# Combining, channel mix and Gram products of a four-layer kernel merged into one stage, with row normalisations on ScalarE

## What is computed

```python
# first layer, end: experts combined, x = res + mo
out = jnp.einsum('ted,te->td', ye, wmat)
# second layer
x_prev = jnp.concatenate([jnp.zeros((B, 1, C), x.dtype), x[:, :-1, :]], axis=1)
xr = mu_r * x + (1.0 - mu_r) * x_prev
xk = mu_k * x + (1.0 - mu_k) * x_prev
r = jax.nn.sigmoid(jnp.einsum('btc,dc->btd', xr, W_r))
k_act = jnp.square(jax.nn.relu(jnp.einsum('btc,dc->btd', xk, W_k)))
out = r * jnp.einsum('btc,dc->btd', k_act, W_v)
# third layer: no softmax, so (q k^T) v = q (k^T v)
attn = jnp.einsum('bhik,bhjk->bhij', q, k)
out = jnp.einsum('bhik,bhkj->bhij', attn, v)
```

## Time and profile before

| | |
|---|---|
| median of three runs | 2536.11 us (2535.68 to 2536.63) |
| the profiled execution: time / span | 2536.58 us / 2534.9 us |
| mean granted TensorE clock | 0.847 of full |
| VectorE busy over the span | 1722.8 us (68%) |
| TensorE busy (matmul) | 1937.0 us (76%) |
| ScalarE busy | 1150.6 us (45%) |
| GpSimd busy | 1454.4 us (57%) |

### The profile page before, as it was taken

How to read it: one execution, slowest core, us unless ns; L and a number is a source line. 1 busy time by engine, 2 the same in 40 slices (tenths; PEclk the granted TensorE clock), 3 DMA queues, 4 the chain that set the end, 5 groups by cost and what they waited for, 6 DMA issues and landing times. The chain is left out here.

```text
span 2534.9 us, 35893 instructions
## 1 busy us (share of the span) xinstructions
PE 1937.0 (76%) x10268; PEld 1496.3 (59%) x10269; DVE 1722.8 (68%) x3375; ACT 1150.6 (45%) x1897; POOL 1454.4 (57%) x1018
## 2 busy tenths in 40 slices
PE   6787868696978788786399999903977686599980
PEld 2445555454545454555399999902665575599970
DVE  1788888888888888885744444466942697644438
ACT  2676767677676768674123232212511452111112
POOL 1789899899989898986133333221211440255542
PEclk9887979697978878797599999956987797699995
DMA  2111111111111111110511111151000012222216
GB/s 73 34 34 47 35 46 36 45 31 40 44 35 44 30 52 30 47 35 21 222 45 47 48 48 48 40 171 47 1 17 11 1 34 96 102 70 69 68 58 198
DMA packets 77370, 139.12 MB, mean 55 GB/s; under 512 B 10449, under 2 KB 48465, under 8 KB 76450
## 3 DMA queue, kind: packets, MB, share of 16 engines
q1 hardware_dynamic: 63586, 100.19, 11.9%
q0 software_dynamic: 13632, 37.24, 4.6%
HBM read 105.38 MB, written 32.01 MB: 54 GB/s over the span
## 5 line engine op out<-in xcount | busy, mean ns | idle before, releaser
L778 DVE TENSOR_TENSOR_SCAN a_hs<-a_dA,a_carry,a_hs 128x512 f32<-128x512 f32 x512 | 637.1, 1268 | 27.7 <-POOL a_hs L400 24.1
L400 POOL TENSOR_TENSOR a_hs<-a_u,a_b_bc 128x1024 f32<-128x1024 f32 x258 | 624.6, 2423 | 0.4
L924 PE MATMUL a_h_ps<-k_ident,a_hs 128*128 128x128 f32 x2064 | 341.1, 318 | 183.7 <-DVE a_hs L778 113.4
L924 PEld LDWEIGHTS a_h_ps<-k_ident,a_hs 128*128 128x128 f32 x2064 | 284.0, 164 | 302.4 <-DVE a_hs L778 136.2
L554 ACT ACTIVATE a_dA<-a_delta,a_a_neg 128x512 f32<-128x512 f32 x512 | 351.8, 688 | 105.0 <-DVE a_hs L778 102.6
L412 POOL TENSOR_TENSOR a_acc<-a_acc,a_part 128x512 f32<-128x512 f32 x242 | 323.6, 1337 | 70.1 <-ACT a_part L568 68.9
L743 DVE SCALAR_TENSOR_TENSOR a_acc<-a_h_ps,a_c_tok,a_acc 128x512 f32<-128x512 f32 x242 | 177.4, 733 | 109.1 <-PE a_h_ps L924 109.0
L568 ACT ACTIVATE a_part<-a_h_ps,a_c_tok 128x512 f32<-128x512 f32 x242 | 165.7, 685 | 149.8 <-PE a_h_ps L924 133.6
L1224 POOL DMA_INDIRECT expert_rows<-m0e_ys,k_pair x71 | 74.1, 1044 | 236.2 <-DVE m0e_ys L1280 225.1
L1290 DVE TENSOR_TENSOR m0e_hT<-m0e_gs,m0e_u 128x512 f32<-128x512 f32 x70 | 48.2, 688 | 185.3 <-ACT m0e_gs L1243 185.3
L1243 ACT ACTIVATE m0e_gs<-m0e_g 128x512 f32<-128x512 f32 x71 | 42.4, 597 | 268.2 <-PE m0e_u L1321 268.2
(11 more groups left out here) (431 smaller groups left out, 3779.0 us busy)
## 6 DMA issues: line engine op xcount, KB each, us to landing
a_b_bc<-b_rows SPq DMA_DIRECT2D x132, 256.0 KB, 3.2
q_y<-expert_rows SPq DMA_DIRECT2D x32, 512.0 KB, 5.6
a_xl<-in_L_attn_x SPq DMA_DIRECT2D x9, 512.0 KB, 3.5
norm_rows<-a_shared SPq DMA_DIRECT2D x9, 512.0 KB, 2.9
m0w_up<-in_m_up SPq DMA_DIRECT2D x1, 4096.0 KB, 12.2
m0w_gate<-in_m_gate SPq DMA_DIRECT2D x1, 4096.0 KB, 22.5
m0w_down<-in_m_down SPq DMA_DIRECT2D x1, 4096.0 KB, 32.2
q_xl<-in_L_attn_x SPq DMA_DIRECT2D x8, 512.0 KB, 3.5
```

Of the source, the lines that this page charges most:

```text
L400: pool.tensor_tensor(hs[n % NBUF][:, half, :], u[s][:, half, :], b_bc[:, n % NBUF:n % NBUF + 1, :].broadcast_to([P, 2, T]), ALU.mult).then ...
L778: dve.tensor_tensor_scan(hs[k][:, c, :], dA[c][:], hs[k][:, c, :], carry[:, hf, c, n:n + 1], ALU.mult, ALU.add).then_inc(s_scan, 1)
L924: last = pe.transpose(hT_ps[j % 2][:, c * P:(c + 1) * P], hs[(n - 1) % NBUF][:, c, j * P:(j + 1) * P], ident[:])
```

## The change

The combining, the channel mix and the Gram products become one stage, `mix_phase`, a written-out pipeline of 13 iterations. Iteration n combines unit n, adds it to x in n+1, transposes and mixes unit n-2, makes the products of unit n-3, and the Gram product of unit n-5. Work moves between engines:

- The weighting of the first expert's rows goes from VectorE to ScalarE (w1 y1) and GpSimd (+ H, 128x1024). The weighted sum of the second stays on VectorE.
- The normalisation for the transposes and that for the Gram products go from VectorE to ScalarE, as scale times x plus shift; GpSimd makes the shift (`NBx`).
- The difference of neighbouring tokens and the carried column go from VectorE to GpSimd.
- The PSUM tiles are halves; relu, the transposed copy, sigmoid and the multiplication go by halves; the r and v products share the PSUM tiles `v_ps`. `ka`, `sig`, `rc`, `a`, `a2` have one buffer each.
- The Gram sums start and stop with flags, the products of zeros go, and ScalarE copies the Gram matrices; the matrix stage keeps weights, mask and the chain of small products.

The core of the diff:

```diff
-def channel_mix_phase(nc, io, per, x):
...
-def attention_matrix_phase(nc, io, per, x):
+def mix_phase(nc, io, per, x, x_in, G):
+    N = TILES // TJ
+    PER_SEQ = N // B
+    LATE_A, LATE_B, LATE_G = 2, 3, 5
+    NBUF = 3
...
+            for t, n in ((w_r, "w_r"), (w_k, "w_k"), (w_v, "w_v"), (mu, "mu")):
+                sp.dma_start(t[:], io[n]).then_inc(s_w, 16)
+            yv = io["expert_rows"][0:PAIRS * P, :].rearrange("(k t p) d -> p k t d", k=2, p=P)
+            for u in range(N):
+                if u >= NBUF:
+                    sp.wait_ge(s_x["q"], u - NBUF + 1)
+                for k in range(2):
+                    sp.dma_start(y[u % NBUF][:, k], yv[:, k, u * TJ:(u + 1) * TJ, :]).then_inc(s_ld[u % NBUF], 16)
+                if u >= 2:
+                    sp.wait_ge(s_x["q"], u - 1)
+                sp.dma_start(xl[u % 2][:], x_in[:, u * TJ:(u + 1) * TJ, :]).then_inc(s_xl[u % 2], 16)
...
+            def power(out, var):
+                pool.tensor_tensor(out, var, half[:], ALU.pow).then_inc(s_pow, 1)
+                powers[0] += 1
+                pool.wait_ge(s_pow, powers[0])
+            def inverse(k, u):
+                s = u % 2
+                pool.wait_ge(s_mv[k], u + 1)
+                power(rs[k][s][:], v[k][s][:])
+                pool.tensor_tensor(nb[k][s][:], rs[k][s][:], neg[k][s][:], ALU.mult).then_inc(s_rs[k], 1)
+            def final(k, u):
+                t = slice(u * TJ, (u + 1) * TJ)
+                pool.wait_ge(s_v2[k], u + 1)
+                power(per.RS[:, t], xv[k][u % 2][:])
+                pool.tensor_tensor(NBx[:, t], per.RS[:, t], xneg[k][u % 2][:], ALU.mult).then_inc(s_fin[k], 1)
+            def difference(u):
+                s = u % 2
+                if u % PER_SEQ == 0:
+                    pool.wait_ge(s_diff, u + -1) if u >= 2 else None
+                    pool.memset(aT[s][:, :, 0:1], 0.0).then_inc(s_halo, 1)
+                else:
+                    pool.wait_ge(s_aT[1], u)
+                    pool.tensor_copy(aT[s][:, :, 0:1], aT[1 - s][:, :, T:]).then_inc(s_halo, 1)
+                for c in range(DC):
+                    pool.wait_ge(s_aT[c], u + 1)
+                if u >= 1:
+                    pool.wait_ge(s_mix, u)
+                pool.wait_ge(s_halo, u + 1)
+                pool.tensor_tensor(diff[:], aT[s][:, :, 1:], aT[s][:, :, 0:T], ALU.subtract).then_inc(s_diff, 1)
+            for n in range(N + LATE_G):
+                if has(n):
+                    pool.wait_ge(s_y0, n + 1)
+                    pool.tensor_tensor(flat(y[n % NBUF][:, 0]), flat(y[n % NBUF][:, 0]), flat(per.H[:, n * TJ:(n + 1) * TJ, :]),
+                                       ALU.add).then_inc(s_h, 1)
+                if has(n - 1):
+                    final("q", n - 1)
+                if has(n - LATE_B - 1):
+                    final("c", n - LATE_B - 1)
+                if has(n - LATE_A):
+                    difference(n - LATE_A)
+                if has(n):
+                    inverse("q", n)
+                if has(n - LATE_B):
+                    inverse("c", n - LATE_B)
...
+            def normal(out, u):
+                for q, t in enumerate(tiles(u)):
+                    last = act.activation(out[:, q, 0:D], x[:, t, :], ACT.Identity, scale=per.RS[:, t:t + 1], bias=NBx[:, t:t + 1])
+                return last
+            def scale(k, u, r):
+                s = u % 2
+                act.wait_ge(s_rs[k], u + 1)
+                for q in range(TJ):
+                    last = act.activation(r[:, q, :], r[:, q, :], ACT.Identity, scale=rs[k][s][:, q:q + 1], bias=nb[k][s][:, q:q + 1])
+                last.then_inc(s_sc[k], 1)
+            def copy_gram(b):
+                act.wait_ge(s_g, PER_SEQ * (b + 1))
+                for c in range(DC):
+                    act.activation(G[b][:, c, :], g_ps[c][:, 0:D + 1], ACT.Copy).then_inc(s_gc, 1)
+            act.wait_ge(s_c, 2)
+            for n in range(N + LATE_G):
+                ma, mb, g = n - LATE_A, n - LATE_B, n - LATE_G
+                if has(n):
+                    act.wait_ge(s_ld[n % NBUF], 32 * (n // NBUF + 1))
+                    for q, t in enumerate(tiles(n)):
+                        last = act.activation(y[n % NBUF][:, 0, q, :], y[n % NBUF][:, 0, q, :], ACT.Copy, scale=per.top[:, t, 0:1])
+                    last.then_inc(s_y0, 1)
+                if has(ma):
+                    act.wait_ge(s_fin["q"], ma + 1)
+                    normal(a, ma).then_inc(s_a, 1)
+                if has(mb):
+                    if mb:
+                        act.wait_ge(s_vp, 2 * mb)
+                    for c in range(DC):
+                        act.wait_ge(s_k, DC * mb + c + 1)
+                        act.activation(ka[:, c, :], k_ps[c][:], ACT.Relu).then_inc(s_relu, 1)
+                if has(ma):
+                    if ma >= 2:
+                        act.wait_ge(s_mix, ma - 1)
+                        act.wait_ge(s_diff, ma)
+                    for c in range(DC):
+                        act.wait_ge(s_t[c], ma + 1)
+                        act.activation(aT[ma % 2][:, c, 1:], t_ps[c][:], ACT.Copy).then_inc(s_aT[c], 1)
+                if has(mb):
+                    act.wait_ge(s_relu, DC * (mb + 1))
+                    act.activation(ka[:], ka[:], ACT.Square).then_inc(s_ka, 1)
+                    if mb:
+                        act.wait_ge(s_out, 2 * mb)
+                    for h in range(2):
+                        act.wait_ge(s_r, 2 * mb + h + 1)
+                        act.activation(sig[:, 2 * h:2 * h + 2, :], v_ps[h][:], ACT.Sigmoid).then_inc(s_sig, 1)
+                if has(g):
+                    if g == PER_SEQ:
+                        copy_gram(0)
+                    act.wait_ge(s_fin["c"], g + 1)
+                    if g:
+                        act.wait_ge(s_g, g)
+                    normal(a2, g).then_inc(s_a2, 1)
+                if has(n):
+                    scale("q", n, y[n % NBUF][:, 1])
+                if has(mb):
+                    scale("c", mb, rc)
+            copy_gram(1)
...
+            def row_stats(k, u, r):
+                for q in range(TJ):
+                    last = dve.bn_stats(st[:, q, :], r[:, q, :])
+                link(last, padded=True)
+                for q in range(TJ):
+                    last = dve.bn_aggr(agg[:, q, :], st[:, q, :])
+                link(last)
+                dve.tensor_scalar(neg[k][u % 2][:], agg[:, :, 0], -1.0, None, ALU.mult)
+                dve.tensor_scalar(v[k][u % 2][:], agg[:, :, 1], EPS_LN, None, ALU.add).then_inc(s_mv[k], 1)
+            def add(k, u, old, r):
+                t = slice(u * TJ, (u + 1) * TJ)
+                dve.wait_ge(s_sc[k], u + 1)
+                dve.tensor_tensor(flat(x[:, t, :]), flat(old), flat(r), ALU.add).then_inc(s_x[k], 1)
+                dve.wait_ge(s_x[k], u + 1)
+                link.carry_wait()
+                for q, j in enumerate(tiles(u)):
+                    last = dve.bn_stats(st[:, q, :], x[:, j, :])
+                link(last, padded=True)
+                for q, j in enumerate(tiles(u)):
+                    last = dve.bn_aggr(per.MV[:, j, :], st[:, q, :])
+                link(last)
+                dve.tensor_scalar(xneg[k][u % 2][:], per.MV[:, t, 0], -1.0, None, ALU.mult)
+                dve.tensor_scalar(xv[k][u % 2][:], per.MV[:, t, 1], EPS_LN, None, ALU.add).then_inc(s_v2[k], 1)
+            dve.wait_ge(s_w, 64)
+            for n in range(N + LATE_G):
+                ma, mb = n - LATE_A, n - LATE_B
+                if has(n - 1):
+                    u = n - 1
+                    dve.wait_ge(s_xl[u % 2], 16 * (u // 2 + 1))
+                    add("q", u, xl[u % 2][:], y[u % NBUF][:, 1])
+                if has(mb - 1):
+                    u = mb - 1
+                    add("c", u, x[:, u * TJ:(u + 1) * TJ, :], rc[:])
+                if has(n):
+                    b = n % NBUF
+                    dve.wait_ge(s_h, n + 1)
+                    for q, t in enumerate(tiles(n)):
+                        last = dve.scalar_tensor_tensor(out=y[b][:, 1, q, :], in0=y[b][:, 1, q, :], scalar=per.top[:, t, 1:2],
+                                                        in1=y[b][:, 0, q, :], op0=ALU.mult, op1=ALU.add)
+                    link(last, padded=True)
+                    row_stats("q", n, y[b][:, 1])
+                if has(ma):
+                    s = ma % 2
+                    dve.wait_ge(s_diff, ma + 1)
+                    for k, o in enumerate((xr[s], xk[s])):
+                        for c in range(DC):
+                            last = dve.scalar_tensor_tensor(out=o[:, c, :], in0=diff[:, c, :], scalar=mu[:, k, c:c + 1],
+                                                            in1=aT[s][:, c, 0:T], op0=ALU.mult, op1=ALU.add)
+                    last.then_inc(s_mix, 1)
+                if has(mb):
+                    for h in range(2):
+                        dve.wait_ge(s_sig, 2 * mb + h + 1)
```

(64 more changed lines are left out.)

235 lines of the change are left out of this document (60 added, 175 removed).

## The result

The changed kernel takes 2565.84 us (median of four runs, 2564.71 to 2567.45) against 2535.89 for the kernel before (2535.19 to 2536.63): a ratio of 1.0121, 95% interval 1.0108 to 1.0133. The predicted time was 2562.5. The profiled execution's span is 2563.1 us, 28.2 longer than before.

A forecast was written before the change was run, and what follows sets the result against it. A ring of waits through the engines' written orders, 27.9 us per full iteration with clock loss, bounds the merged stage: 256.3 plus 39.7 for the matrix stage is 296.0 against 269.5, giving 2562.5 us, forecast range 2550 to 2576 (0.64).

The forecast's parts named there:

- The ring: Merged stage: a closed chain of waits through the engines' written orders, 25.7 us per full iteration at full clock.
- A: GpSimd makes the inverse deviation and shift after the channel mix's row statistics: 2.3 us, lower end 1.4.
- E: TensorE transposes, then does the r product: 4.8 us with a hand-over, plus 2.2 us for slow clock.
- G: ScalarE normalises for the Gram product, behind the sigmoid: 2.07 us.
- H: TensorE's Gram product for one unit, ahead of the v product in its order: 3.6 us with hand-over.
- Start: Merged stage until first rows are there: 5.5 us plus 1.8 for four weight loads ahead of them, 7.3 us.
- Iterations 0 to 2: Merged stage's first iterations, with only the combining: 11.6 us each, the difference adding 2.4 in the third, 37.2 us.
- Matrix stage: Stage after the merged one: chain of products 31.1 us, exposed loads 5.8, stage switch 0.6, clock 2.2; 39.7 us.
- The clock term: TensorE's idle of about 7 us ahead of the transposes slows them and the r product: 2.2 us per full iteration.
- Clock stays up: Rival: TensorE's clock stays at 2.4 GHz, all clock terms go, 16.4 us less, 2546 us; chance 0.12.
- VectorE held by GpSimd: Rival: GpSimd's additions hold VectorE until it closes the ring itself, 21 us more, 2584 us; chance 0.07.
- Faster: Rival: the ring does not close, busiest engine sets iterations 4 to 10 near 16.5 us, 2501 us; chance 0.09.

The follow-up runs named there:

- experiment 4: Changed kernel with four more row-statistics instructions per unit on VectorE, ahead of the mix: 2564.20 us.
- (3): Changed kernel with one more normalising pass per unit on ScalarE: 2565.80 us beside the r product, 2587.09 us directly ahead of the second normalising.
- experiment 5: Changed kernel with six unused matmuls on TensorE behind the k product, in its idle ahead of the transposes: 2559.20 us.
- the combined kernel: Changed kernel with v product ahead of Gram product, channel-mix scaling one iteration later (VectorE's addition and GpSimd's shift for it moved too), and earlier loads: 2493.71 us.
- experiment 7: Changed kernel with first unit's rows loaded ahead of the mix weights and the matrix stage's six loads issued in the merged stage: 2550.42 us.
- experiment 2: Changed kernel with ScalarE scaling the channel mix's rows one iteration later, behind the normalising for the transposes: 2535.16 us.
- experiment 1: Changed kernel with TensorE issuing the v product ahead of the Gram product in each iteration: 2519.14 us.
- Experiment 6: Changed kernel with the second normalising, for the Gram product, moved back from ScalarE to VectorE: 2547.17 us.
- the one with the dose on VectorE: The combined kernel with four more row-statistics instructions per unit on VectorE: 2501.28 us.

## Why the prediction was right, step by step

**The ring holds.** A cut at either of two places gives 46.7 and 30.7 us back, and a dose costs 21.3 us on the ring and nothing beside it, be it on ScalarE or on VectorE. That one engine's load sets the pace, the rival on the other side, is excluded for the changed kernel: more work on VectorE (experiment 4), on ScalarE beside the ring (3) and on TensorE (5) cost nothing. In the combined kernel VectorE's load does set it, in the turns with all parts: it is busy for 97% of them, and the dose comes through. In the two turns without combining the dose comes through as well (1.3 us), though VectorE waits 5.1 us there, so there it is again its place and not its load.

**Its terms.** A was 2.31 (1799.18 to 1801.49), predicted 2.3. B with hand-over 1.98 (2.07), C 1.60 (1.7), D with hand-over 2.11 (2.07), E 7.1 with the low clock (4.8 and 2.2), F 0.5 (0.65), G with hand-over 2.11 (2.07), H 3.58 (3.6), I with hand-over 3.72 (3.6), J 2.82 (2.85). Iterations 5 to 7 took 83.9 us, predicted 83.7; 8 and 9 52.8 (52.4); 10 21.0 (20.5); iteration 4 20.3 (20.5); the tail 18.7 (18.3).

**What was mis-sized.** *Start*: 9.5 us, predicted 7.3. I had added four issues of DMAs to the old start; the rows also landed later behind the weights, and experiment 7 gave back 4.3. *Iterations 0 to 2*: 35.5 (37.2); I had put the whole 2.4 us of the difference into the third, but it took 1.90 and ran in part beside VectorE's statistics, so that iteration was 1.3 us longer than the second. *Iteration 3*: 15.3 (16.4). *Matrix stage*: 40.0 (39.7), with 34.0 for chain and clock (33.3). That the sum came out within 1 us, 297.0 against 296.0, is in part luck: a start 2.2 us too short and four first iterations 2.8 us too long cancel. Another 0.8 us came from ahead of the stage, which began at 1662.27 and not 1661.45. The other 1.5 of the 3.3 us between forecast and result are medians against profiled executions: I took the median 0.5 below, and it lies 1.0 above.

**The clock term was right in size, but its cause was only half right.** I put 2.2 us per iteration on the idle of 7 us ahead of the transposes, as in the earlier trace rows, and the loss was there: 0.9 for the transposes and 0.5 to 2.1 for the r product. But it doesn't go with that idle. With it mostly filled (experiment 5), the loss moved, in two of three units, to the Gram product behind an idle of 2.65 us (5.42 instead of 3.74); with 5.40 us ahead of the Gram product (experiment 2) it was there too, and with 4.02 us of idle (experiment 1) it stayed at the transposes. While TensorE pauses elsewhere in the turn, filling one pause doesn't give the price back: it returned 6.6 us and not 18. Which pause costs in which unit stays open.

**The rivals.** *Clock stays up*: no, 0.77 granted over the stage. *VectorE held by GpSimd*: it is held, by 1.9 us in the iteration shown (1.37 and 0.90 for two instructions of 0.17) and not by up to 4.7, and in its slack, as argued against it. The changed kernel shows on VectorE

```profile
1783.32 1.37 DVE L1749 TENSOR_SCALAR c_neg_q<-c_agg 128x4 f32<-128x4 f32 x1
```

an instruction that takes 0.17 alone, and that ends with GpSimd's subtraction. Once VectorE set the pace, such holds were in it: two of them add 1.6 us to the combined kernel's iteration of 17.9. *Faster*: its place was named wrongly. I wrote that with G early enough for H not to wait the units would fall to VectorE's 16.5. Experiment 6 made G early, the wait fell to 0.60, and the spacing to 25, because H itself lay on the ring. The 16.5 were nearly reached (17.9, with 1.6 of holds in it) only when H, and then the scaling, were taken off it.

**ScalarE's price.** Experiment 6 moved one normalising back to VectorE, as the rule of the Trainium skill (ScalarE: Activation LUTs, Rules for kernel authors) would have it. It took 2.4 to 3.9 us off each of five spacings here, more than the 0.7 between 2.07 and 1.37 us: what paid was the place in the order. With the ring cut the same step made the spacings longer, by 6.0 us together. The rule goes by what an instruction costs on each engine; here the written orders decided on which of them it should stand.

**Open.** A's hold (1.92 for a power that takes 1.01 alone) was not tried apart, nor the first normalising on VectorE, nor what the holds of VectorE cost in the combined kernel.

## What to carry to other kernels

When stages are merged into one with a written order per engine, walk the orders from one engine's item to the next until you are back at the start: an iteration takes at least the sum of that ring, however idle the engines are, and only where the ring is shorter does the busiest engine set the time. Here one exchange of two blocks on TensorE was worth 47 us, where the merge as written lost 30. Put first in each order what somebody waits for soonest; nobody waited for the Gram product within its iteration. A dose of some 2 us on an engine at two places of its order tells whether its load or its place counts.

## What the runs showed of the hardware

**A one-input VectorE instruction waits for GpSimd too.** 128x4 `tensor_scalar` instructions took up to 1.59 us where 0.17 is usual, in the rows looked at each time until a GpSimd operation of 1024 columns ended; in the combined kernel:

```profile
1758.90 2.36 POOL L1664 TENSOR_TENSOR c_y<-c_y,k_hidden 128x1024 f32<-128x1024 f32 x1
...
1759.70 1.59 DVE L1767 TENSOR_SCALAR c_xneg_q<-k_mean_var 128x4 f32<-128x4 f32 x1
```

VectorE's row statistics, also of one input, ran beside the same addition at their usual 0.41. The Trainium skill (SBUF — State Buffer, Who interferes with whom) says that `tensor_scalar` can enter a mode that takes the ports shared with GpSimd, and that the one who comes second is blocked for the whole instruction; this trace agrees, 1.42 us for four columns. The instruction's size doesn't show what it can cost.

**The clock can fall in a chain without a pause.** Behind its first start the matrix stage's chain of products ran without an idle that the timeline marks, both in the combined kernel and in the one with the dose on VectorE. The same two late products, in the first kernel and (second fence) in the second:

```profile
1872.48 2.07 PE L1933 MATMUL g_q<-g_t,y_w_vT 128*128 128x256 f32 x4
...
1876.48 5.30 PE L1933 MATMUL g_q<-y_w_oT,g_vk 128*128 128x256 f32 x16
```
```profile
1882.02 1.13 PE L1939 MATMUL g_q<-g_t,y_w_vT 128*128 128x256 f32 x4
...
1884.14 3.72 PE L1939 MATMUL g_q<-y_w_oT,g_vk 128*128 128x256 f32 x16
```

Both chains begin alike, with a first group of 3.69 us, and only in the first do the products get slower later, from 1868.95 on. The granted clock over the chain is 0.83 in the first and 1.00 in the second. The first chain takes 30.9 us to the next stage's first load, the second 26.1, with the same instructions and no edit there. Why it fell in one and not in the other is not shown. So two kernels can differ by 5 us in a place that neither touched, here 0.2% of the time; compare the stage that was edited before you compare the totals.
